# Order of work in the last odd pair and in the first quads, and an add moved from VectorE to GpSimd

## What is computed

```python
q_emb = relu(q @ W3 + b3)
x1 = (n * v + sum(v, axis=1)) * q_emb[:, None, :]        # n = 512 tokens
y = relu(x1 @ W2 + b2)                                   # L0_cond
base_out = y @ W_base + b_base
shared_out = (y @ A_s) @ B_s
gates = softmax(y @ W_router + b_router)                 # top 2 of 6 kept
routed_out = (h * w_per_e) @ B_r,  h = y @ A_r
out = x + base_out + shared_out + routed_out
```

## Time and profile before

| | us |
|---|---|
| median of 3 runs | 1385.65 |
| lowest and highest | 1385.61, 1387.47 |
| the profiled execution, its own time | 1386.83 |
| its span in the profile | 1385.0 |
| TensorE busy | 1371.7 (99%) |
| VectorE busy | 1146.0 (83%) |
| ScalarE busy | 707.8 (51%) |
| GpSimd busy | 106.0 (8%) |

### The profile page before, as it was taken

The page is one execution under the profiler, slowest core; times in us unless marked ns, Lnnn a source line. Parts: engine busy times, 40 slices in busy tenths (PEclk is TensorE's granted clock), DMA queues, the critical chain, the costliest instruction groups (busy, mean ns, idle before and its releaser), DMA issues.

```text
span 1385.0 us, 18647 instructions
## 1 busy us (share of the span) xinstructions
PE 1371.7 (99%) x5997; PEld 1122.0 (81%) x5997; DVE 1146.0 (83%) x1835; ACT 707.8 (51%) x1262; POOL 106.0 (8%) x214
## 2 busy tenths in 40 slices
PE   9999999999999999999899999999999999999998
PEld 5888887888888888888778888888888888888887
DVE  6977788878887887978889757889898878988797
ACT  7774766558565676656554233454333433334231
POOL 2000111010010101100000000110010100101000
PEclk9999999999999999999999999999999999999999
DMA  8153765757356563564855729969697584957845
GB/s 320 63 181 111 236 221 176 226 169 218 100 148 202 167 217 95 162 214 135 284 197 155 240 89 321 349 203 330 224 320 250 179 300 141 350 200 224 285 149 201
DMA packets 160786, 289.21 MB, mean 209 GB/s; under 512 B 41424, under 2 KB 41680, under 8 KB 160688
## 3 DMA queue, kind: packets, MB, share of 16 engines
q1 hardware_dynamic: 135344, 199.23, 43.4%
q0 software_dynamic: 20592, 74.98, 17.9%
q10 hardware_dynamic: 4752, 13.80, 2.5%
HBM read 197.90 MB, written 90.05 MB: 208 GB/s over the span
## 4 chain that ended last, share of the span: by engine, by line
PE 90%; DMA 3%; DVE 3%; issue 1%; ACT 1%; SPq 0%; DVEq 0%; POOL 0%; ACTq 0%; POOLq 0%
PE ps L3403 30%; PE ps L3405 30%; PE ps L3404 30%; DMA wh_raw<-in_wbase 1%; DMA inner_scratch<-staged 1%; DVE act_lo L2118 1%; DVE buf L2186 1%; PE ps L3414 1%; DMA inner_w<-inner_scratch 0%; DMA partner<-y_scratch 0%; DMA buf<-in_xT 0%; DVE staged L2407 0%; PE ps L3429 0%; DVE act_lo L2547 0%; SPq L861 0%
## 5 line engine op out<-in xcount | busy, mean ns | idle before, releaser
L3403 PE MATMUL ps<-act_hi,w_hi 128*128 128x512 f32 x1312 | 511.3, 390 | 0.0
L3404 PE MATMUL ps<-act_lo,w_hi 128*128 128x512 f32 x1312 | 511.2, 390 | 0.0
L3405 PE MATMUL ps<-act_hi,w_lo 128*128 128x512 f32 x1312 | 511.1, 390 | 0.0
L3403 PEld LDWEIGHTS ps<-act_hi,w_hi 128*128 128x128 f32 x1312 | 246.7, 188 | 52.3 <-DVE act_lo L2111 0.9
L3405 PEld LDWEIGHTS ps<-act_hi,w_lo 128*128 128x128 f32 x1312 | 246.7, 188 | 51.6
L3404 PEld LDWEIGHTS ps<-act_lo,w_hi 128*128 128x128 f32 x1312 | 246.5, 188 | 51.4
L3403 PE MATMUL ps<-act_hi,inner_w 128*128 128x512 f32 x420 | 164.3, 391 | 2.2 <-DMA inner_w<-inner_scratch 1.4
L3405 PE MATMUL ps<-act_hi,inner_w 128*128 128x512 f32 x420 | 163.5, 389 | 0.0
L3404 PE MATMUL ps<-act_lo,inner_w 128*128 128x512 f32 x420 | 163.4, 389 | 0.0
L1157 ACT ACTIVATE act_hi<-src 128x512 fp32r<-128x512 f32 x184 | 108.6, 622 | 98.2 <-PE ps L3405 94.1
L2118 DVE TENSOR_TENSOR act_lo<-src,act_hi 128x512 fp32r<-128x512 f32 x168 | 110.4, 685 | 9.9 <-ACT act_hi L1157 9.5
(11 more groups left out here) (199 smaller groups left out, 1885.3 us busy)
## 6 DMA issues: line engine op xcount, KB each, us to landing
src<-in_xT SPq DMA_DIRECT2D x224, 256.0 KB, 4.3
inner_w<-inner_scratch POOLq DMA_DIRECT2D x105, 512.0 KB, 4.5
src<-y_scratch SPq DMA_DIRECT2D x128, 256.0 KB, 5.5
y_scratch<-buf SPq DMA_DIRECT2D x116, 256.0 KB, 3.3
outT<-buf SPq DMA_DIRECT2D x103, 256.0 KB, 4.6
inner_scratch<-staged ACTq DMA_DIRECT2D x21, 512.0 KB, 5.4
wl_raw<-in_wbase SPq DMA_DIRECT2D x8, 1024.0 KB, 7.1
inner_scratch<-staged POOLq DMA_DIRECT2D x14, 512.0 KB, 5.2
```

The costliest lines, as they stand in the source:

```text
L3403: nc.tensor.matmul(out, wh, a_h, start=start, stop=False, skip_group_check=onto)
L3404: nc.tensor.matmul(out, wh, a_l, start=False, stop=False, skip_group_check=onto)
L3405: return nc.tensor.matmul(out, wl, a_h, start=False, stop=stop, skip_group_check=onto)
```

## The change

It has these parts.

1. In the last odd pair of the stage of W2 SP issues the loads of quadrants Q21 and Q22 before the last store of C12 and the store of `hw`, not after them, and the loads of Q11 and Q12 after the third store of C22, not after the second.
2. There VectorE does `y_low(C12, 3)`, `c22(1)` and `c22(2)` ahead of `wb_sum_1`; the `y_low` of C22 and `low(8, 0, k)` come ahead of `wb_sum_2`, whose four instructions stand together behind `c21(2)`, and the four `wb_low(1, k)` stand at the end. ScalarE's `y_high(C22, 0)` moves ahead of `wb_high(3, k)` and its `wb_high(2, k)` behind all of `high(8, 0, k)`.
3. In the first quad of the stage of W2 `t3(i, 2)` and `t3(i, 3)` come after `add_u4`, not before `inner_low(r, 6)`.
4. In the first quad of the stage of W_base `inner_weight_low(3 * L2 + 3)` comes after the first `inner_low`, not before the pair's end.
5. In the six joined pairs of the stage of W_base the 24 instructions of `u4_add_x` leave VectorE, and GpSimd does the same add (`add_x22`), four instructions behind the last weight load of each of the runs 4 and 6.

```diff
--- before.py
+++ after.py
@@ -659,13 +659,13 @@
                         store_gates(i - 1, GA)
                     if k > 0 and not joined(i):
                         store_c12(k - 1)
-                store_c12(H - 1)
-                if joined(i):
-                    store_hw(i - 1, GB)
                 if last:
                     sp.wait_ge(bank_done, group_no(i, 2, H - 1))
                     load_quadrant(wl_raw[:, 2], Q21, wl_loaded[2])
                     load_quadrant(wh_raw[:, 2], Q22, wh_loaded[2])
+                store_c12(H - 1)
+                if joined(i):
+                    store_hw(i - 1, GB)
                 last_stores(i)
 
             def joined_loads(i):
@@ -709,7 +709,7 @@
                         sp.dma_start(y_dram[2 * i + 1, H + k - 1], buf3[:, k - 1, :]).then_inc(buf3_stored[k - 1], 16)
                         if i == 0:
                             load_next(0, G12, k - 1)
-                    if k == 2 and last:
+                    if k == 3 and last:
                         sp.wait_ge(wb_sum, H)
                         load_quadrant(wh_raw[:, 2], Q11, wh_loaded[2])
                         sp.wait_ge(y_used, y_no(i - 1, C12, H - 1))
@@ -1086,7 +1086,15 @@
 
             for k in range(L2):
                 store_weights(WB_P1, k)
+            def add_x22(p, j):
+
+                pool.wait_ge(u4_copied, four(NP + p, j))
+                pool.wait_ge(x_loaded[tile(G12, j)], loads(NP + p, G12, 2))
+                nc.gpsimd.tensor_tensor(buf3[:, j, :], src[:, tile(G12, j), :], buf3[:, j, :],
+                                        ALU.add).then_inc(x22_added, 1)
+
             for e in range(EARLY, len(QUADS)):
+                p = QUADS[e] - NP
                 begin(RUN[e, 1])
                 if e == EARLY:
                     load_partner(e)
@@ -1094,6 +1102,9 @@
                     if n > 1:
                         begin(RUN[e, n])
                     stream(RUN[e, n])
+                    if n > 1:
+                        for j in range(H):
+                            add_x22(p + (n == 6), j)
 
         @block.scalar
         def _(act):
@@ -1661,13 +1672,14 @@
                     for j in range(H):
                         wb_high(1, j)
                     y_high(i, C12, 3)
+                    y_high(i, C22, 0)
                     for j in range(H):
                         wb_high(3, j)
-                    y_high(i, C22, 0)
                     for j in range(H):
                         high(i + 1, 0, j)
                         if j < H - 1:
                             y_high(i, C22, j + 1)
+                    for j in range(H):
                         wb_high(2, j)
                     return
                 y_high(i, C12, 1)
@@ -2703,11 +2715,17 @@
                 inner_low(r, 5)
                 if first:
                     inner_weight_low(L2 + 6)
-                for j in range(H):
-                    t3(i, j)
+                t3(i, 0)
+                t3(i, 1)
+                if not first:
+                    t3(i, 2)
+                    t3(i, 3)
                 inner_low(r, 6)
                 add_u4(r, 0)
                 add_u4(r, 1)
+                if first:
+                    t3(i, 2)
+                    t3(i, 3)
                 gate_weights(i - 1, GB)
                 for j in range(H):
                     low(i, 3, j)
@@ -2832,20 +2850,37 @@
                     c22(i, 0)
                     low(i, 6, 2)
                     low(i, 6, 3)
+                    y_low(i, C12, 3)
+                    c22(i, 1)
+                    c22(i, 2)
                     for j in range(H):
                         wb_sum_1(j)
-                    y_low(i, C12, 3)
-                    c22(i, 1)
+                    y_low(i, C22, 0)
+                    c22(i, 3)
                     wb_low(3, 0)
                     wb_low(3, 1)
-                    c22(i, 2)
+                    y_low(i, C22, 1)
                     wb_low(3, 2)
                     wb_low(3, 3)
-                    c22(i, 3)
-                    y_low(i, C22, 0)
                     gate_apply(i - 1, GA)
-                    wb_low(1, 0)
-                    wb_low(1, 1)
+                    low(i + 1, 0, 0)
+                    y_low(i, C22, 2)
+                    low(i + 1, 0, 1)
+                    c21(i, 0)
+                    t1(i + 1, 0)
+                    low(i + 1, 0, 2)
+                    y_low(i, C22, 3)
+                    c21(i, 1)
+                    low(i + 1, 0, 3)
+                    t1(i + 1, 1)
+                    c21(i, 2)
+                    for j in range(H):
+                        wb_sum_2(j)
+                    t1(i + 1, 2)
+                    t1(i + 1, 3)
+                    for j in range(H):
+                        wb_low(1, j)
+                    return
                 else:
                     y_low(i, C12, 1)
                     low(i, 6, 0)
@@ -2860,22 +2895,12 @@
                     c22(i, 3)
                     y_low(i, C22, 0)
                     gate_apply(i - 1, GA)
-                if last:
-                    wb_sum_2(0)
                 for j in range(H):
                     low(i + 1, 0, j)
-                    if j > 0 and last:
-                        y_low(i, C22, j)
-                        c21(i, j - 1)
-                    elif j > 0:
+                    if j > 0:
                         c21(i, j - 1)
                         y_low(i, C22, j)
                     t1(i + 1, j)
-                    if last and j < H - 1:
-                        wb_sum_2(j + 1)
-                if last:
-                    wb_low(1, 2)
-                    wb_low(1, 3)
 
             def alone1(i):
                 c21(i - 1, H - 1)
@@ -3056,6 +3081,8 @@
                 inner_low(r, 0)
                 if e > EARLY:
                     c21_of(p - 1, 3)
+                else:
+                    inner_weight_low(3 * L2 + 3)
                 inner_t1(r)
                 inner_low(r, 1)
                 inner_t2(r)
@@ -3140,17 +3167,13 @@
                 inner_low(f, 5)
                 if first:
                     inner_weight_sums(WB_P6)
-                u4_add_x(p, 0)
                 if first:
                     inner_weight_low(4 * L2 + 3)
-                u4_add_x(p, 1)
                 if first:
                     inner_weight_low(4 * L2 + 4)
                 inner_low(f, 6)
                 add_u4(f, 0)
                 add_u4(f, 1)
-                u4_add_x(p, 2)
-                u4_add_x(p, 3)
                 c22_of(p, 0)
                 lr_low_d(p)
                 if first:
@@ -3316,8 +3335,6 @@
                     if g == SECOND - 1 and j == 1:
                         inner_weight_low(3 * L2 + 2)
                         inner_weight_sums(WB_P4)
-                    elif g == SECOND - 1 and j == 2:
-                        inner_weight_low(3 * L2 + 3)
 
             def pair2(p):
                 g = NP + p
```

## The result

The changed kernel takes 1389.28 us (median of 7 runs, 1388.59 to 1391.9), against 1385.65 us of the kernel before (7 runs beside it). The ratio is 1.0028, with a 95% interval of 1.0017 to 1.0039: it is slower, by 3.9 us with an interval of 2.4 to 5.4. The forecast was 1386.2 us and "no change".

What follows compares the result with a forecast made beforehand. TensorE, busy 99%, was taken as the bound, with about 10 of 1385 us winnable in its gaps. Terms 0.1 + 0 - 0.6 + 1.1 + 0 = +0.6 on the median 1385.65 gave 1386.2 us; range 1381.4 to 1389.6.

Steps and rivals of the forecast that it cites:

- The sum: Whole kernel: all terms together +0.6 us on the median of 1385.65, no change; chance 0.52.
- the rivals: Whole kernel, four other outcomes: 1381.6 us (chance 0.26), 1389.8 (0.10), 1388.7 (0.09), up to 1388 (0.03).
- The last odd pair: Last odd pair, stage of W2: -1.7 us from the waits, +1.8 for the clock, +0.1 in all; bounds -3.4 and +1.9.
- One wait instead of three: Last odd pair: TensorE waits once before C21, from 698.3 to 705.4, 7.1 us long, 1.7 us ahead of before.
- 0.2 us to spare: Last odd pair: TensorE's other two waits go as well, the tightest by 0.2 us.
- The clock term: Last odd pair: the low granted clock behind TensorE's one wait costs 1.8 us, as before; at most twice that.
- I take 0: Stage of W_base: GpSimd's adds free 14 us of VectorE and change the time by 0, at the dear end +1.5.
- that rival: Stage of W_base: each GpSimd add blocks VectorE, 26 to 38 us in all; +2 to +3, 1388.7 us; chance 0.09.
- VectorE's remainders longer while GpSimd adds: Stage of W_base: a profile sign that would show the forecast wrong; no size given.

Runs made afterwards that it cites:

- e1: The kernel before with only the 24 adds of x moved to GpSimd: 1387.11 us, ratio 1.0011.
- e5: The kernel before with the change's last-odd-pair orders, plus y_low of C21(0) to (2) and c21(3) ahead of wb_sum_2, wb_high(2, k) last: 1382.49 us, ratio 0.9978.
- e4: The kernel before with only inner_weight_low moved behind the first inner_low: 1387.57 us, ratio 1.0009.
- e7: As e5, and on SP the last store of C22 ahead of the second pair of loads, C21's stores ahead of the third: 1378.39 us, ratio 0.9948.

## Where the forecast held and where it failed

The sum was +0.6 us and the changed kernel lost 3.9. That the time still lies in the range is owed to the rivals, which had pushed its upper end to 1389.6. One of them named the right cause for the largest part of the loss; the sum had put that part at nothing.

**The last odd pair: right in its path, the clock's cost too small.** One wait instead of three, before C21(0), was expected to last from 698.3 to 705.4. With 1.2 us taken off for the chance at 226, that is 697.1 to 704.2; it began at 698.06 and ended at 704.09. It began late because of the wait of 0.46 us before C22(0) at 684.12, where the forecast had 0.2 us to spare. The store of C12(3) was expected at 679.7 and came at 679.05, the last `y_low` of C22 was to wait for its store until 695.1 and began at 693.54 (both with the 1.2 still to be taken off). VectorE after, for the earlier trace rows:

```profile
679.05 0.69 DVE L2256 SCALAR_TENSOR_TENSOR buf_lo<-buf,yhi 128x512 fp32r<-128x512 f32 x1 [3.63 <-DMA y_scratch<-buf]
...
693.54 0.69 DVE L2256 SCALAR_TENSOR_TENSOR buf_lo<-buf,yhi 128x512 fp32r<-128x512 f32 x1 [1.54 <-DMA y_scratch<-buf]
```

The clock term was 1.8 and is 2.8: it was taken from before, where the waits are shorter, and where the slow matmuls between 696.7 and 699.7 come to 1.6. The stretches that answer to the earlier trace rows:

```profile
680.00:700.00 20.00, 17.61 (x77) 13.88 (x75) 18.46 (x31) 8.80 (x16) 0.00 (x0) 1.00 0.98 340
700.00:710.00 10.00, 5.91 (x14) 4.64 (x15) 10.00 (x18) 4.02 (x8) 0.00 (x0) 0.66 0.40 120
704.09:710.31 6.22, 6.22 (x15) 4.87 (x16) 6.22 (x11) 0.63 (x1) 0.00 (x0) 0.53 0.66 198
```

Fifteen matmuls take 6.22 us behind the wait, 3.4 at full clock. So the pair came out at +0.9 and not +0.1 in these two traces, and at -0.4 us (-1.5 to +0.8) as measured alone: within what was forecast.

**Part 3: right**, 0.

**Part 4: right in mechanism.** The load of `ha` was expected at 885.1, went at 884.79 and took 7.6 us to land where 7.5 was taken; its loss at TensorE was to be 1.1 and is 0.9 (0.59 in the row and some pipeline filling), the gain at `inner(r, 0)` 0.6 and is 0.7. That is +0.2 in this trace where +0.5 was forecast; alone the part measured 1.2 us (0 to 2.5) above before, and that stays open.

**Part 5: the step that failed.** "I take 0" rested on two things: that none of TensorE's waits behind 905 names VectorE, and that GpSimd's own time has cover. Both held for what they say. What was left out is what VectorE loses while GpSimd works: it was weighed as a rival, with a chance of 0.09 and 1388.7 us, and that rival is what the chip did; "VectorE's remainders longer while GpSimd adds" stood among the signs of being wrong. The rival's blocking of 26 to 38 us is 26.7 in the trace, but it put the price at the `c22` of three pairs, where one pair and the end of the program pay. That its 1388.7 us comes near the measured 1389.28 is in part luck, as the other parts of the loss (0.9 in the last odd pair, 0.5 by chance) aren't in it. The forecast itself counted 14 us freed on VectorE, where the trace shows 10 more. VectorE's idle time hides most of that, but not where VectorE runs without a pause from the hold to the tight `c22` (at 957.44 to 973.74 in the changed kernel), and once more at the end of the program, where the stores have no work behind them to hide in. 26.7 us of holding cost 0.7 us in one place and 0.8 in the other (0.7 and 1.1 in `e1`).

The Trainium skill ("SBUF — State Buffer", "Who interferes with whom") says that a VectorE instruction with two SBUF inputs contends with a GpSimd instruction that reads SBUF, and that one with at most one such input does not (outside the two-port modes). The runs agree in both halves: 1.22 us became 5.92, and 0.75 with one operand in PSUM stayed 0.75. From the 4497 ns for 2048 columns in the Trainium skill ("GPSIMD Engine Reference", "3.1 Elementwise — side-by-side cycle accounting") the forecast had estimated 1.1 us for an add; the trace has 1.29.

What stays open: part 5 alone costs 1.5 us (0.3 to 2.6), while the changed kernel and the one without part 5 lie 3.2 apart (about 1.0 to 5.4). The intervals allow the same number for both; whether the parts make each other worse was not told apart.

## What to carry to other kernels

Before work is moved to GpSimd, look at what VectorE reads meanwhile: where its next instruction had two operands in SBUF, each add cost VectorE 1.1 to 1.2 us of standing still instead of its own 0.6 to 0.7, and the move freed nothing; the instructions with one operand in PSUM lost nothing beside an add. Where several waits of one engine have one cause, a new order that serves the first of them may only gather them in the next place: here it took the order of three queues (VectorE's, ScalarE's and SP's) to clear the pair, and VectorE's and ScalarE's order alone won two fifths of it. And before a wait of 1 us in one trace is explained, look whether it is in a second trace at all.

## What was not expected of the hardware

- Four GpSimd adds in a row hold one VectorE instruction through all four (5.92 us for 1.22): it gets no turn between them.
- What a wait of TensorE costs in clock behind it can't be told from its length alone. In the last odd pair the longer wait cost more: after waits of 5.8 to 6.1 us (three kernels) 2.8 to 3.0 us were lost to a granted clock of 0.50 to 0.66 between 700 and 710; after one of 4.4 us 1.7, at 0.83; and after one of 2.4 us (`e5`) nothing. But in the same trace of `e5` a shorter wait, of 1.8 us before 225.69, is followed by eight matmuls at half speed, 1.6 us lost; 1.4 us of waiting in the same place cost nothing in before. The stretch in `e5`, granted clock 0.66:

```profile
226.00:231.00 5.00, 5.00 (x16) 3.95 (x15) 2.27 (x6) 0.64 (x2) 2.15 (x4) 0.66 0.75 213
```

- The two or three waits of before's order in that pair, 1.3 to 4.3 us each, cost about 1.6 in all in six traces, behind the first or behind the last of them, and nothing in the seventh (`e4`, where the matmuls keep their 0.23 us; its granted clock was recorded only as a mean). Between them TensorE worked at the level of 2.4 GHz or, behind the waits, at 1.2.
- The same load landed so differently that its wait at TensorE was 1.4 us in the trace of before and between 0 and 1.8 in the others, with no part of the change to go by.
- A store of 256 KB landed 9.0 us after its issue behind 4 MB of loads (`e5`) and 4.4 us where 2 MB of them stood behind it (`e7`).
